# A mixture-of-experts loop in float32: the transposes of the slot rows two pairs ahead, placed behind the second half of the next up product on TensorE

## What is computed

```python
def swiglu5(h, alpha, gate_scale, up_shift, gate_clamp_raw, up_clamp_raw):
    g = jnp.clip(h[..., ::2], -gate_clamp, gate_clamp)
    u = jnp.clip(h[..., 1::2], -up_clamp, up_clamp)
    return g * jax.nn.sigmoid(g * alpha) * gate_scale * (u + up_shift)
...
w, idx = jax.lax.top_k(gate_probs, K)
...
he = jnp.einsum('nd,edh->enh', xf, expert_w1) + expert_b1[:, None, :]
te = swiglu5(he, ...)
oe = jnp.einsum('enh,ehd->end', te, expert_w2) + expert_b2[:, None, :]
y = jnp.einsum('ne,end->nd', cw, oe)
```

## Time and profile before

| | us |
|---|---|
| median of 3 runs | 2351.46 |
| lowest and highest of them | 2348.83 and 2352.56 |
| the profiled execution | 2351.67 |
| its span, first to last instruction | 2349.9 |
| TensorE busy in the span | 2328.6 |
| VectorE, GpSimd, ScalarE busy | 1394.8, 996.4, 913.9 |

### The profile page before, as it was taken

The page is one execution under the profiler, slowest core; times in us unless marked ns, Lnnn a source line. Parts: engine busy times, 40 slices in busy tenths (PEclk is TensorE's granted clock), DMA queues, the critical chain, the costliest instruction groups (busy, mean ns, idle before and its releaser), DMA issues. The chain is left out here.

```text
span 2349.9 us, 27693 instructions
## 1 busy us (share of the span) xinstructions
PE 2328.6 (99%) x9585; PEld 1433.2 (61%) x9585; DVE 1394.8 (59%) x2436; ACT 913.9 (39%) x1530; POOL 996.4 (42%) x1356
## 2 busy tenths in 40 slices
PE   8999999999999999999999999999999999999999
PEld 4565655457676657777556777665767755544443
DVE  8777860524875663777554587555477655623445
ACT  5346642222764211666121376321266522312221
POOL 2005211142655331565342365442266533637775
PEclk9999999999999999999999999999999999999999
DMA  6411010320666210466210176510056611679517
GB/s 182 141 35 33 25 47 28 114 82 15 158 169 189 78 59 1 108 168 159 81 44 23 37 176 162 139 44 23 1 145 167 165 54 54 221 244 345 187 46 238
DMA packets 132363, 257.69 MB, mean 110 GB/s; under 512 B 49695, under 2 KB 51471, under 8 KB 129884
## 3 DMA queue, kind: packets, MB, share of 16 engines
q1 hardware_dynamic: 85294, 150.84, 21.9%
q0 software_dynamic: 45584, 102.75, 15.8%
q10 hardware_dynamic: 1346, 2.33, 0.3%
HBM read 213.17 MB, written 32.20 MB: 104 GB/s over the span
## 5 line engine op out<-in xcount | busy, mean ns | idle before, releaser
L115 POOL DMA_DIRECT2D cols<-w x720 | 352.9, 498 | 248.5 <-PE psum L785 201.8
L785 PE MATMUL psum<-cols,rows 125*128 125x256 f32 x1600 | 369.0, 379 | 0.0
L772 PE MATMUL psum<-g_k_cols,g_q_cols 128*125 128x512 f32 (+1 forms) x960 | 360.8, 513 | 0.2
L785 PEld LDWEIGHTS psum<-cols,rows 125*128 125x128 f32 x1600 | 303.1, 190 | 39.5 <-issue 3.8
L882 DVE CUSTOM_DVE_ANT_0 g_prob<-psum,ln_count 125x1250 f32<-125x1250 f32 x160 | 233.8, 1461 | 102.9 <-PE psum L772 102.6
L772 PEld LDWEIGHTS psum<-g_k_cols,g_q_cols 128*125 128x125 f32 x960 | 179.4, 187 | 165.2 <-issue 155.5
L967 ACT ACTIVATE g_prob<-g_prob,g_row_max 125x1250 f32<-125x1250 f32 x160 | 215.7, 1348 | 125.0 <-DVE g_row_max L882 123.1
L896 DVE STREAM_TRANSPOSE w<-g_prob 128x1280 f32<-128x1280 f32 x160 | 241.5, 1509 | 38.0 <-DMA cols<-w 23.6
L973 ACT ACTIVATE g_prob<-g_prob,g_row_max 125x1250 f32<-125x1250 f32 x160 | 215.5, 1347 | 67.2 <-DVE g_row_max L871 66.9
L3011 PE MATMUL psum<-m_ew,m_x_cols 128*64 128x256 f32 (+1 forms) x576 | 150.0, 491 | 0.0
L843 PE MATMUL psum<-w,g_k_cols 128*125 128x512 f32 x320 | 143.6, 592 | 0.0
(11 more groups left out here) (408 smaller groups left out, 4013.7 us busy)
## 6 DMA issues: line engine op xcount, KB each, us to landing
cols<-w POOLq DMA_DIRECT2D x720, 80.0 KB, 3.2
cols<-w SPq DMA_DIRECT2D x560, 80.0 KB
w<-in_L_gnn_m_w SPq DMA_DIRECT2D x8, 1024.0 KB
slot_rows<-p_kf SPq DMA_DIRECT2D x1, 7344.0 KB, 32.6
rows<-slot_rows SPq DMA_DIRECT2D x54, 136.0 KB
m_ew<-in_L_ffn_expert_w SPq DMA_DIRECT2D x4, 1536.0 KB, 12.8
slot_outputs<-slot_rows SPq DMA_DIRECT2D x1, 5000.0 KB
w<-in_L_mix_W SPq DMA_DIRECT2D x4, 1024.0 KB, 5.2
```

What stands on the lines that cost most here:

```text
L115: return eng.dma_start(out, in_, allow_slow_non_contiguous=True)
L772: ins = pe.matmul(psum[0:P, at:at + width], q_cols[:, h, t * P:(t + 1) * P], k_cols[:, h, start:start + width], start=True, stop=True)
L785: ins = pe.matmul(c.bank(6 + g % 2, 256).rearrange("p (u a i) -> p u a i", u=2, a=SIDE), rows[0:P, j, h * 128:(h + 1) * 128], turned_keys[ ...
```

## The change

In `experts_pe` the call that turns the slot rows of pair i+2 stood behind the turns of gate i and ahead of the second part of up i+1. It now stands behind that second part and ahead of the down product of pair i.

```diff
                     ins = pe.transpose(psum[0:128, at:at + 128], gate[u][:, k * 128:(k + 1) * 128], ident[:, :])
                 ins.then_inc(turned, 1)
-                if i + 2 < PAIRS:
-                    turn_slots_pe(i + 2)
                 if 0 < i < PAIRS - 1:
                     up_pe(i + 1, BANK, 2 * FFN_I - BANK)
                 elif i:
                     hot_pe(0, 3)
+                if i + 2 < PAIRS:
+                    turn_slots_pe(i + 2)
                 pe.wait_ge(t_made, i + 1)
                 if i >= 1:
                     pe.wait_ge(out_made, i)
```

## The result

The changed kernel takes 2357.49 us (median of 8 runs, 2355.53 to 2358.75); the kernel before took 2351.90 beside it (8 runs, 2348.83 to 2354.95). The ratio is 1.0021, with an interval of 1.0012 to 1.0031: slower by 5.6 us, between 2.8 and 7.3. Now and then an execution runs at a much lower clock (one of the kernel before took 3533 us), and such executions are left out of all medians and ratios here. In the profiled execution the time is 2355.98 us for a span of 2354.2, which is 4.3 more than before (predicted: 4.0).

The account below looks back on a forecast made before the run. TensorE, busy 2328.6 of 2349.9 us, was taken as the bound. Form changes cost 7.3 us, shrunken waits give part back, net +4.0: 2351.67 + 4.0 = 2355.7, stated as 2355.5 us, range 2351.0 to 2359.6.

Parts of the forecast that it names:

- The price: Each added excursion on TensorE from 64-column form into 128-column turns and back costs 0.30 to 0.31 us; 7.3 in all.
- The sizes of the single borders: At TensorE's form changes: 0.10 us too much into the turns, 0.14 out of them, 0.06 at the second matmul behind.
- Rival 2: TensorE loads weights ahead across the form border, so the excursion costs nothing and waits remain: 2351.5 us; chance 0.11.
- So gate 7 stays at 2158.17: Store landing that releases VectorE at pair 7 does not move; TensorE's waits at pairs 6 and 7 shrink 2.3 to 0.5 us.
- near 2160: Sign of being wrong: gate 7 on TensorE near 2160 instead of still at about 2158.
- Rival 1: VectorE's store wait at pair 7 slides along with TensorE, so the whole price is seen: +7.3 us, 2358.8; chance 0.28.
- I take the full clock: Behind pair 7's 0.5 us idle time TensorE's clock does not drop: gate 8 at 2167.3 instead of 2168.60.
- Pair 9 then gets a wait: VectorE awaits a store issued behind pair 7: gate 9 not before 2177.0, where TensorE alone would be there at 2176.4.
- The sum: Profiled execution 2351.67 us plus 4.0 gives 2355.7; the runs' median being 0.2 lower, 2355.5 us was forecast.
- The other engines: 0: ScalarE's later row copy (0.6 us) stays covered, VectorE starts 0.44 us earlier per pair, the tail follows TensorE: no cost.

## Why the prediction was right, and where not

**The price: right.** 0.30 to 0.31 per excursion was predicted and 0.30 measured, in three cadences. The sizes of the single borders (0.10 in, 0.14 and 0.06 out) came out as 0.10, 0.15 and 0.05. Rival 2, no price, is refuted by the 9.10. The rule of the Trainium skill (TensorEngine Tiling (Array Packing), section Key Properties), that a switch of tiling mode drains the engine, agrees with these numbers, which show the lost time and not the drain itself. The Trainium skill's rule on loads pulled ahead (TensorE: Matmul & The Clock Gate, section Step-by-step: what each phase is for) holds within a form (the load for the up matmul of 2269.75 starts at 2269.54), and not at a border, where the load starts with its matmul.

**"So gate 7 stays at 2158.17": off by 0.9 in the first profile, right in the second.** The step took the landing of the kernel before for that of the changed one. Counted from gate 1, the wait was to be 0.5 us; it was 1.47 in one profile and 0.66 in the other. By the clock of the first profile gate 7 came at 2159.81, which is what the prediction had named as a sign of being wrong ("near 2160"); 0.70 of that is the later gate 1. Rival 1 said that the landing may slide by up to 1.8 us and decides from a slide of 0.7 on. It slid 0.9 once, and yet the whole price was not seen, because TensorE is 1.8 us later by itself at gate 7, which still takes 0.9 from the wait, because the clock did not drop (1.6), and because the 0.4 near pair 17 are gone.

**"I take the full clock": right, in part by luck.** Both profiles of the changed kernel show 1.00 behind gate 7, and both of the kernel before a stretch at 1.2 GHz there, worth 1.6 to 1.7 us (gate 8 after 10.43 and 10.49). The reason given was an idle time of 0.5 us. In the first profile it was 1.39, and other executions show that idle times not much longer can go either way, as told below.

**"Pair 9 then gets a wait": a wrong place, a right size.** The first profile has none, since gate 7 and with it TensorE was already 0.9 later; the second has 0.21 at gate 9 and 0.25 at gate 10, against 0.64 predicted. What held VectorE at pair 9 before was a guess: the profile names no releaser there ("issue"). In both profiles of the changed kernel it names the store.

**The sum.** Predicted +7.3 and -3.3, net 4.0. The two profiles of the changed kernel, against the one the prediction started from: +7.2 (24 x 0.30), and waits of 1.47 and 1.12 instead of 4.36, so -2.9 and -3.2: net 4.31 and 3.96. The ratios say 5.6 both times (2352.02 x 0.0024 in the second session), with intervals that reach down to 2.8 and 3.1, so 4.0 lies within both and whether the typical run loses more than the profiled ones stays open. It would, if some runs of the kernel before had less to give back than these two profiles with 4.2 to 4.4 us of waits and slow clock. There are such runs by the granted clock: in the last session 11 of 29 runs of before have a mean of 1.000, with a median of 2350.86, and 15 have 0.999, with one of 2352.90. No such run was profiled.

**The other engines: 0. Right** for ScalarE (copy over 2.1 us early). For VectorE and GpSimd it was right in the sum, but there is more in it. GpSimd's list is the longer one, as its stores in the kernel before show (timeline of GpSimd):

```profile
2232.95 1.04 POOL L3210 DMA_INDIRECT slot_outputs<-m_work,m_slot_place  x1 [0.30 <-issue]
...
2241.99 1.04 POOL L3210 DMA_INDIRECT slot_outputs<-m_work,m_slot_place  x1 [0.30 <-issue]
```

9.04 us apart, with nothing but pauses of 0.3 and 0.56 us between its instructions: more than TensorE's 8.80. From the store of pair 10 to that of pair 22 it is 9.08 us a pair on average in this profile and 9.12 in the second, which is about the 9.10 of the changed kernel. So GpSimd falls behind in the order before; in the second profile of it the distance from a store to the bias step that needs it shrinks from 11.2 us at pair 11 to 7.1 at pair 25. In the changed kernel it stays at 11.05 from pair 13 to 20, with the stores 9.10 apart. A store takes 2.8 to 15.4 us from issue to landing in the changed kernel (median 4.1), so this lag costs nothing on its own once the DMA engines are less full. But with the store first GpSimd's period goes up to 9.3, with the waits one step longer its loads start later, and on both of these bases the median of the changed order is no higher than that of the old one (3.7 and 0.5 us lower). By the intervals of the ratios such a difference is known to about 3.5 us, so the runs exclude there the 5.6 us of the plain kernels, not a smaller loss. The prediction looked at GpSimd for a slide that would keep the waits; what was to be seen there was that the slower order gives it room. The step from the period to the medians is argued, not shown, and on the second base the profiles speak against it (4.2 us between the gates).

## What to carry to other kernels

Count how often TensorE's instruction stream changes between array forms, not only how many instructions it holds: here each round trip between 64-column pairs and 128-column turns cost 0.30 us, and blocks of one form belong together. Before an engine's list is reordered, ask whose pace the stage really has: of the 7.2 us of price, 4.1 to 4.3 were seen in the profiles, since waits gave the rest back. And do not carry a wait over from one profile to a changed kernel to the tenth of a us: two executions of the changed kernel had the same landing 0.8 us apart.

## What the runs showed of the hardware that was not expected

*The length of an idle time alone does not decide whether the clock drops.* TensorE sat idle ahead of a gate for 1.97, 2.12 and 1.84 us in three executions and then ran for some 3 us at 1.2 GHz; it sat idle for 2.22, 2.06 and 1.81 us in others and stayed at 2.4 GHz. Ahead of the down product, with the places on VectorE, it dropped behind 2.34 and 3.24 us and stayed up behind 2.67, 3.01, 3.03 and 3.07 us. Three windows at half clock (kernel before, kernel before again, and the changed order with waits one step longer; columns as above):

```profile
2159.00:2161.00 2.00, 2.00 (x10) 1.20 (x11) 0.00 (x0) 1.06 (x2) 1.28 (x5) 0.50 1.01 413
```

```profile
2164.00:2166.00 2.00, 2.00 (x12) 1.17 (x10) 0.00 (x0) 0.37 (x1) 1.30 (x4) 0.50 1.04 435
```

```profile
2161.00:2163.00 2.00, 2.00 (x13) 1.08 (x11) 0.00 (x0) 0.18 (x1) 1.45 (x2) 0.50 0.92 373
```

and two that kept it, behind idle times of 2.22 and 2.06 us (order before, waits one step longer):

```profile
2149.00:2153.00 4.00, 3.71 (x29) 2.38 (x31) 0.23 (x1) 1.02 (x2) 3.10 (x3) 1.00 1.03 414
...
2179.00:2183.00 4.00, 3.72 (x29) 2.39 (x31) 0.22 (x1) 1.02 (x2) 3.08 (x4) 1.00 0.75 192
```

What else decides stays open. For a forecast it means: an idle time between 1.8 and 3.2 us may or may not bring a stretch at 1.2 GHz; behind a gate it cost some 1.6 us.

*A signal of TensorE can be seen late.* Between the start of the last matmul of the second part and VectorE's bias step lie 0.43 us when nothing disturbs. In the first profile of before it is 0.65 to 2.6 us in most pairs from 9 on, though the profile names the store at none of them (TensorE's signal at most, no engine or an unnamed one at five) and TensorE's own matmuls ran on at 8.80; in the second profile of the same kernel it is 0.43 from pair 11 on; in both profiles of the changed kernel too. With the store first it is 2.4 to 2.9 us in seven pairs. From pair 12 to 17 of the first profile, and in those seven, the bias step starts 0.1 to 0.4 us behind the end of GpSimd's cast (2244.09 behind 2243.77, for instance); at other pairs it is late without such a neighbour, and in the changed kernel it starts 0.18 us behind the cast in eight pairs (12 to 19) without being late. The largest cases are ScalarE's: with the places on VectorE its copy of the turned gate came 4.7 to 6.0 us behind the turns six times, against 0.58 elsewhere, and each time it held TensorE up. All six fall into the only places where GpSimd issues ten to twelve DMAs in a row with pauses of 0.3 us (it is six in most pairs of those kernels), and the copy starts 1.3 to 1.7 us behind the end of the last of them. That points at the run of DMA issues, but nothing tested it: the cause is open.

*A float32 product with the identity costs twice the transposing instruction:* 0.22 us (two halves of 64 columns side by side) against 0.11 us for a block of 128 by 128, with two instructions for each half instead of one for the block.
